# Attention sums of a two-layer graph attention in the next layer's layout: four heads side by side, weight sums repeated over 32 rows

## The chip, the cores and the metric

One Trainium2 chip, one core. The metric is the device time of one execution in microseconds, as the median over runs; lower is better.

## The reference, cut to what matters

Four graphs of 256 nodes go through two graph-attention layers of 8 heads with 32 outputs each, then through a gated residual sum, a layer norm, a router (2 of 16 experts per token) and a mixture of experts with one shared expert.

```python
def gat_layer(x, adj, W, a_self, a_neigh, b):
    feat = jnp.einsum('nf,hfo->hno', x, W)
    e = attn_self[:, :, None] + attn_neigh[:, None, :]
    e = jax.nn.leaky_relu(e, 0.2) + MASK_VAL * (1.0 - adj)[None, :, :]
    alpha = jax.nn.softmax(e, axis=-1)
    out = jnp.einsum('hnm,hmo->hno', alpha, feat) + b[:, None, :]
    return jax.nn.elu(jnp.transpose(out, (1, 0, 2)).reshape(out.shape[1], -1))
...
x = x + jnp.tanh(g_xattn[0]) * gat(gat(ctx, ...), ...)
x = x + jnp.tanh(g_ffn[0]) * moe(_layernorm(x))
```

The softmax's division is made late: the kernel sums weight times feature and weight alone, and divides the one by the other. The elu follows.

## The kernel before, in words

All orders are written out by hand, engine by engine; semaphores join them. A **unit** k is one graph in one layer; `UNITS` lists the four graphs in layer 0 (k = 0 to 3), then the four in layer 1 (k = 4 to 7). The stretch over all units is called the graph stage here. In a unit VectorE makes the terms of 8 heads (`edge(k, h)`, L857, two instructions a head, 128x256 each) out of `ps_edge` into `prob`, a ring of 4 heads. Between two heads `task(k, h)` puts small jobs for the unit before, for the one after, and for the routing of graphs that are done. TensorE has a like order (`task(k, j)`, j counts pairs of heads):

- `edges` (L1198) makes the sums for VectorE's next pair of heads; `rows` (L1165) and `features` (L1174, L1178) belong to units ahead; `spread_t` is L1187.
- `weighted(k, j)` (L1214) sums the terms of two heads. The weights' sum is a 33rd column of `feat`, so a head takes 33 columns of the array; one head stands at column 0 and the other at column 64.
- `turn_pv` (L1225) turns the sums of all heads, after ScalarE (`evict_pv`, L582) has copied them out of `ps_pv`. VectorE's `normalise` takes 16 reciprocals per row (L865) and multiplies (L868); ScalarE's `elu` (L592, L594) and VectorE's `add_elu` (L875) follow. In layer 0 the result is turned again (`turn_z`, L1143 on `att`) and copied out to `h1_t` (`evict_h1`); in layer 1 it is added to `x_res` (L879).

GpSimd multiplies features (L438), takes differences (L423, L461) and later scatters rows (L488) and results (L496). After the graph stage come the routing of the last graphs (`norm_stats`, `hat`, `turn_hat`, `high`, `low`, `route`, `top_two`, `hot`, `ranks`, `positions`), half of the shared expert's steps (`up` L1306, `down` L1316), the table of tiles (`tables`), 31 tiles of routed tokens (L1335, L1346, L1362), the other half of the shared steps, and the collection of results: `bring` (L1063) adds them, `base` (L1029) adds the shared part, and for graph 3 TensorE adds them (L1325).

Of the kernel before, what the change touches and what calls it, by code (L numbers as in the profile page):

```python
# [9 lines left out]
ALU = mybir.AluOpType  # L10
# [3 lines left out]
P = 128  # L14
# [20 lines left out]


def flamingo_block(nc, x, ctx_t, gates, w0, w1, a_self, a_neigh, b0, b1, router_t, router_bias,
# [24 lines left out]
    y_view = [y_tok[Y_SLOTS * P + k * TOKENS:Y_SLOTS * P + (k + 1) * TOKENS, :].rearrange(  # L62
        "(g t p) d -> g p t d", g=B, p=P) for k in range(TOP)]

    with ExitStack() as ctx:
# [6 lines left out]
        def sem(name):  # L72
# [70 lines left out]
        pv_t = sb("pv_t", [P, PAIRS, N])  # L143
        inv_sum = sb("inv_sum", [P, T, HEADS])
# [41 lines left out]


# [13 lines left out]
        y_sb = pv_t  # L201
        y_got = [t[:].rearrange("p a c n -> p (a c n)").rearrange("p (a t d) -> p a t d", a=B, t=T)
                 for t in (prob, mask_t)]
# [6 lines left out]
        ps_mix = ps_nat[:, 0, :]  # L210
        ps_route = ps_feat[:].rearrange("p c f -> p (c f)")
# [13 lines left out]
        down_landed = sem("down_landed")  # L225
# [21 lines left out]
        pv_zeroed, edge_ready, p_done, pv_done = (sem("pv_zeroed"), sem("edge_ready"), sem("p_done"),  # L247
                                                  sem("pv_done"))

        pv_out, pv_turned = [sem(f"pv_out{i}") for i in range(2)], sem("pv_turned")  # L250
        elu_exp = sem("elu_exp")
        z_done, elu_act, elu_sum, z_turned, h1_ready = (sem("z_done"), sem("elu_act"), sem("elu_sum"),
                                                        sem("z_turned"), sem("h1_ready"))
# [20 lines left out]
        y_landed = [[sem(f"y_landed{k}{g}") for g in range(B)] for k in range(TOP)]  # L274
        last_added = sem("last_added")
# [22 lines left out]
        def _(sp):  # L298
# [48 lines left out]
            sp.dma_start(down_w[:, 0:EXPERTS, :], wd).then_inc(down_landed, 16)  # L347
            sp.dma_start(down_w[:, EXPERTS:STEPS, :], sd).then_inc(down_landed, 16)

# [21 lines left out]
            for g in range(B):  # L371
                sp.dma_start(y_got[0][:, g], y_view[0][g]).then_inc(y_landed[0][g], 16)
# [6 lines left out]
        def _(pool):  # L379
# [46 lines left out]
            def scale_features(k):  # L426
# [8 lines left out]
                if k >= 2:  # L435
                    pool.wait_ge(pv_done, PAIRS * (k - 1))
# [3 lines left out]
                                   ).then_inc(feat_ready, 1)  # L440

# [8 lines left out]
            def name_rows(a):  # L450
# [3 lines left out]
                if a == B - 1:  # L454
                    pool.wait_ge(pv_done, PAIRS * NU)
# [51 lines left out]
            for k in range(NU):  # L507
                if graph_after(k - 2, 1) is not None:
                    norm_rstd(graph_after(k - 2, 1))
# [961 lines left out]
```

## Time and profile before

| | us |
|---|---|
| median of 3 runs | 228.59 (228.13 to 230.41) |
| the profiled execution | 228.06 |
| its span | 226.3 |
| graph stage, first to last term of VectorE | 18.46 to 123.53 |
| tiles, from their first turn | 158.35 |
| last instruction of `base` begins | 222.96 |

The span is what the profile covers; 1.76 us of the execution lie around it. In rows of the trace an instruction is given with its line, what it writes and reads, its shape and its time; a PE row's shape begins with the array's rows and columns that it uses.

### The profile page before, as it was taken

What the parts mean: (1) busy time and instruction counts of PE and PEld (TensorE: products, weight loads), DVE (VectorE), ACT (ScalarE), POOL (GpSimd) and SP (SyncE); (2) the same over time, 40 slices, a digit from 0 to 9 for tenths busy, and PEclk for the clock granted to TensorE, in tenths of its full rate; (3) what the DMA queues carried; (4) which work ended last, traced back from release to release, by engine and by line L of the source; (5) the groups of instructions that cost most, each with busy time, mean ns of one, the idle gap of its engine ahead of it and who ended that gap; (6) DMA issues with size and microseconds to landing.
All of it is one profiled execution on the core that took longest, in us unless ns stands there. A gap on an engine that the chain in (4) does not pass through costs nothing.

```text
span 226.3 us, 4159 instructions
## 1 busy us (share of the span) xinstructions
PE 187.1 (83%) x1106; PEld 139.9 (62%) x1106; DVE 167.1 (74%) x506; ACT 116.5 (51%) x313; POOL 109.6 (48%) x140
## 2 busy tenths in 40 slices
PE   0267999899999998698896879288899999999943
PEld 0245555556676666285463679277799999987910
DVE  6946997897979788957997675764677777772455
ACT  2075646958647685564505443000588888885200
POOL 8616771861141847544656235670056666667000
PEclk9999557999999999978558576659999999999995
DMA  3899999999940040880001002225245665642484
GB/s 114 223 242 407 426 424 427 418 433 421 316 138 1 3 139 0 243 311 6 1 23 70 0 3 93 72 93 136 55 133 171 189 184 180 184 136 89 139 295 152
DMA packets 20616, 40.13 MB, mean 177 GB/s; under 512 B 2769, under 2 KB 16658, under 8 KB 18418
## 3 DMA queue, kind: packets, MB, share of 16 engines
q1 hardware_dynamic: 17250, 32.64, 41.5%
q0 software_dynamic: 2256, 6.18, 7.8%
q10 hardware_dynamic: 1088, 1.05, 1.4%
q8 instruction: 10, 0.16, 0.3%
q14 instruction: 12, 0.10, 0.1%
HBM read 15.59 MB, written 24.27 MB: 176 GB/s over the span
## 4 chain that ended last, share of the span: by engine, by line
PE 59%; DVE 19%; ACT 8%; issue 8%; DMA 4%; POOL 0%; DVEq 0%; ACTq 0%; POOLq 0%
PE ps_pv L1214 11%; PE ps_edge L1346 10%; PE ps_pv L1362 6%; DVE prob L857 5%; PE ps_edge L1306 4%; PE ps_edge L1198 4%; PE ps_rows L1165 4%; PE ps_nat L1225 3%; PE ps_pv L1316 3%; PE ps_nat L1143 3%; PE ps_nat L1335 3%; DMA mask_t<-y_tok 3%; PE ps_feat L1178 2%; DVE att L875 2%; PE ps_nat L1187 1%
## 5 line engine op out<-in xcount | busy, mean ns | idle before, releaser
L857 DVE SCALAR_TENSOR_TENSOR prob<-ps_edge,t_nat,mask_t 128x256 f32<-128x256 f32 x128 | 53.7, 474 | 4.1 <-PE ps_edge L1198 1.3
L1214 PE MATMUL ps_pv<-prob,feat 128*33 128x256 f32 x256 | 40.6, 446 | 4.3 <-DVE prob L857 4.2
L496 POOL DMA_INDIRECT y_tok<-pv_t,y_row x31 | 29.7, 959 | 27.6 <-issue 14.6
L461 POOL TENSOR_TENSOR up_lo<-up_raw,up_hi 128x512 fp32r<-128x512 f32 x18 | 23.1, 1296 | 15.1 <-ACT up_hi L619 15.1
L1346 PE MATMUL ps_edge<-up_hi,sel_row 128*128 x124 | 25.9, 301 | 0.8 <-DVE sel_row L1036 0.8
L1214 PEld LDWEIGHTS ps_pv<-prob,feat 128*33 128x33 f32 x256 | 13.8, 123 | 19.1 <-issue 6.6
L1198 PE MATMUL ps_edge<-rows_r,sel_row 128*128 128x256 f32 x64 | 18.0, 374 | 5.5 <-DVE prob L857 5.4
L1198 PEld LDWEIGHTS ps_edge<-rows_r,sel_row 128*128 128x128 f32 x64 | 11.4, 227 | 14.7 <-DVE prob L857 9.0
L1036 DVE TENSOR_TENSOR sel_row<-ps_nat,sel_row 128x256 fp32r<-128x256 f32 x31 | 13.1, 424 | 9.1 <-ACT sel_row L700 9.1
L1346 PEld LDWEIGHTS ps_edge<-up_hi,sel_row 128*128 128x128 f32 x124 | 18.8, 189 | 1.6 <-issue 1.6
L1362 PE MATMUL ps_pv<-down_w,x_less 128*128 x62 | 18.6, 383 | 0.0
L1346 PE MATMUL ps_edge<-up_lo,sel_row 128*128 x62 | 17.4, 280 | 0.0
L423 POOL TENSOR_TENSOR rows_r<-rows_e,rows_h 128x256 fp32r<-128x256 f32 x8 | 5.8, 729 | 23.7 <-ACT rows_h L551 23.7
L582 ACT ACTIVATE pv_t<-ps_pv 128x512 f32<-128x512 f32 x16 | 9.6, 598 | 13.4 <-PE ps_pv L1214 13.4
L718 ACT ACTIVATE pv_t<-ps_pv,mask_t 128x256 f32<-128x256 f32 x31 | 14.7, 474 | 3.3 <-PE ps_pv L1362 0.3
L488 POOL DMA_INDIRECT x_rows<-x_hat,pos x12 | 11.9, 993 | 8.2 <-DVE pos L955 5.4
L1165 PE MATMUL ps_rows<-xc_t,w_rows 65*128 65x256 f32 x16 | 6.9, 578 | 9.8 <-DVE w_rows L812 9.8
L694 ACT ACTIVATE a_all<-ps_edge 128x256 f32<-128x256 f32 x8 | 3.0, 380 | 20.0 <-PE ps_edge L1306 20.0
L700 ACT ACTIVATE sel_row<-ps_nat 128x256 fp32r<-128x256 f32 x31 | 11.6, 378 | 2.5 <-PE ps_nat L1335 2.5
L438 POOL TENSOR_TENSOR feat<-feat_raw,feat 128x512 f32<-128x512 f32 x8 | 8.6, 1073 | 8.5 <-ACT feat_raw L568 8.2
L706 ACT ACTIVATE mask<-ps_edge 128x128 f32<-128x128 f32 x31 | 8.6, 277 | 7.4 <-PE ps_edge L1346 7.4
L1225 PEld LDWEIGHTS ps_nat<-ident,pv_t 128*128 128x128 f32 x64 | 9.0, 172 | 5.3 <-issue 5.3
(186 smaller groups left out, 476.3 us busy)
## 6 DMA issues: line engine op xcount, KB each, us to landing
x_rows<-x_hi SPq DMA_DIRECT2D x16, 1024.0 KB, 22.8
mask_t<-x_rows SPq DMA_DIRECT2D x31, 129.0 KB, 2.1
down_w<-in_wd SPq DMA_DIRECT2D x1, 2048.0 KB, 9.3
up_raw<-in_wu SPq DMA_DIRECT2D x5, 384.0 KB, 6.9
up_raw<-in_wg SPq DMA_DIRECT2D x5, 384.0 KB, 8.0
x_res<-in_x SPq DMA_DIRECT2D x4, 256.0 KB, 3.4
prob<-y_tok SPq DMA_DIRECT2D x4, 256.0 KB, 4.6
mask_t<-y_tok ACTq DMA_DIRECT2D x4, 256.0 KB, 6.8
```

Source lines behind the costliest of these rows:

```text
L461: pool.tensor_tensor(up_lo[:, e], up_raw[:, e % RAW_SLOTS], up_hi[:, e].bitcast(F32), ALU.subtract).then_inc(up_ready, 1)
L488: pool.indirect_dma_start(x_rows[:], bass.IndirectOffsetOnAxis(pos[:, a, k, t:t + 1], 0), rows_of[a][:, k, t, :], None).then_inc(scattered ...
L496: pool.indirect_dma_start(y_tok[:], bass.IndirectOffsetOnAxis(y_row[:, j % R_SLOTS:j % R_SLOTS + 1], 0), y_sb[:, j % Y_SLOTS, :], None).th ...
L718: act.activation(y_sb[:, j % Y_SLOTS], ps_y[j % 2], ACT.Copy, scale=x_in[:, j % X_SLOTS, D + 1:D + 2]).then_inc(y_ready, 1)
L857: last = dve.scalar_tensor_tensor(prob[:, n % 4, c, :], ps_edge[n // 2 % 2][:, h % 2, :], t_nat[:, k % 2, c, 0, h:h + 1], mask_t[:, a, c, ...
L1036: dve.tensor_tensor(xt_lo[:, j % 2], ps_xt[j % 2], xt_hi[:, j % 2].bitcast(F32), ALU.subtract).then_inc(lo_done, 1)
L1165: last = pe.matmul(ps_rows[:, side], w_rows[i][:, c, side, :], src, start=(c == 0), stop=(c == chunks - 1))
L1198: last = pe.matmul(ps_edge[n % 2][:, h % 2, :], sel_row[:, h, :], rows_r[:, k % 2, :], start=True, stop=True)
L1214: last = pe.matmul(ps_pv[at:at + HO, j, :], feat[:, k % 2, c, h, :], prob[:, (HEADS * k + h) % 4, c, :], start=(c == 0), stop=(c == C - 1))
L1225: last = pe.transpose(ps_nat[:, t, j * P:(j + 1) * P], pv_t[:, j, t * P:(t + 1) * P], ident[:])
L1346: last = pe.matmul(to, m[:, j % 2, c, :], w[:, bass.ds(e, 1), :, c * P:(c + 1) * P], start=(i == 0), stop=(i == len(todo) - 1))
L1362: pe.matmul(ps_y[j % 2], ht_r[:, j % 2], down_w[:, bass.ds(e, 1), :], start=True, stop=True).then_inc(y_done, 1)
```

## The change

Four heads stand side by side at columns 0, 32, 64 and 96 (`sums(k, q)`, q counts groups of four). Features' sums and weights' sums become two sets of matmuls; the weights' column is repeated 32 times, so that each weight sum comes out in the same 32 rows as the feature sums that it divides. Nothing is turned: ScalarE copies the feature sums (`evict_sums`), VectorE takes the reciprocal of the whole block of weight sums (`invert`), and GpSimd multiplies the two (`weigh_sums`). For the last unit VectorE does both, in two halves (`normalise_last`). The elu is now max(x, exp(-relu(-x)) - 1) in layer 0, written straight into `h1_t` (`next_layer`), and exp(-relu(-x)) + relu(x) in layer 1, where the two parts are turned and added by TensorE (`turn_elu`) and the -1 stays in `less_gate` as before.

The terms now have 8 places: the second four lie in the half of `down_w` that holds experts 8 to 15, which is loaded only when the last sums are made. The orders of all engines move with this. After the graph stage `norm_stats(2)`, `shared_step(0)`, `positions`, `top_two_in(3)`, `up(1)`, `down(0)` and the scatter of graph 1 change places. Each token's two results lie side by side in `y_tok`, so that one transfer of 512 KB brings a graph's results, and TensorE adds those of graphs 2 and 3.

```diff
+QUAD = 4
+LATE_DOWN = (8, 16)
...
+        terms = [prob[:], down_w[:, LATE_DOWN[0]:LATE_DOWN[1], :].rearrange("p (a c) n -> p a c n", c=C)]
...
+            sp.wait_ge(quad_done, 2 * NU)
+            sp.dma_start(down_w[:, LATE_DOWN[0]:LATE_DOWN[1], :], wd[:, LATE_DOWN[0]:LATE_DOWN[1], :]
+                         ).then_inc(late_down_landed, 16)
...
+            def weigh_sums(k):
+                pool.wait_ge(inv_ready, k + 1)
+                pool.wait_ge(f_sum_out, k + 1)
...
+                pool.tensor_tensor(z[:], f_sum, w_inv, ALU.mult).then_inc(z_done, 1)
...
+            def elu(k, halves=slice(0, 2)):
...
+                act.activation(att[:, halves], z[:, halves], ACT.Relu, scale=-1.0).then_inc(elu_step, 1)
...
+                last = act.activation(att[:, halves], att[:, halves], ACT.Exp, scale=-1.0)
+                if UNITS[k][1] == 1:
+                    last = act.activation(z[:, halves], z[:, halves], ACT.Relu)
...
-            def normalise(k):
-                dve.wait_ge(pv_turned, k + 1)
-                pv = ps_nat[:].rearrange("p t (h o) -> p t h o", h=HEADS)
-                link(dve.reciprocal(inv_sum[:].unsqueeze(3), pv[:, :, :, F_OUT:HO]))
...
+            def invert(k):
+                dve.wait_ge(quad_done, 2 * k + 2)
...
+                dve.reciprocal(w_inv, ps_weight).then_inc(inv_ready, 1)
+            def normalise_last(half):
...
+                link(dve.reciprocal(w_inv[:, half], ps_pv[:, 2 * half + 1]))
+                dve.tensor_tensor(z[:, half], ps_pv[:, 2 * half], w_inv[:, half], ALU.mult).then_inc(z_done, 1)
+            def next_layer(k):
...
+                dve.scalar_tensor_tensor(h1_t[:, a % 2], att[:], -1.0, z[:], ALU.add, ALU.max).then_inc(h1_ready, 1)
...
+            def sums(k, q):
+                pe.wait_ge(p_done, HEADS * k + QUAD * (q + 1))
...
+                for c in range(C):
+                    for h in heads:
+                        at = F_OUT * (h % QUAD)
+                        last = pe.matmul(ps_pv[at:at + F_OUT, to_f, :], feat[:, k % 2, c, h, 0:F_OUT], terms[q][:, h % QUAD, c, :],
+                                         start=(c == 0), stop=(c == C - 1))
+                last.then_inc(sums_done, 1)
...
+                for c in range(C):
+                    for h in heads:
+                        at = F_OUT * (h % QUAD)
+                        last = pe.matmul(ps_pv[at:at + F_OUT, to_w, :],
+                                         feat[:, k % 2, c, h, F_OUT:HO].to_broadcast([P, F_OUT]),
+                                         terms[q][:, h % QUAD, c, :], start=(c == 0), stop=(c == C - 1))
+                last.then_inc(quad_done, 1)
...
+            def turn_elu(k, a):
...
+                        pe.matmul(to, att[:, g, t * P:(t + 1) * P], ident[:], start=True, stop=False)
+                        last = pe.matmul(to, z[:, g, t * P:(t + 1) * P], ident[:], start=False, stop=True)
```

VectorE, unit 3, before: its heads, the next unit's row maxima, and the jobs of unit 2 between heads.

```order
L857 SCALAR_TENSOR_TENSOR prob<-ps_edge0,t_nat,mask_t 128x256 x2
L838 TENSOR_REDUCE row_max<-ps_rows 128x2
L857 SCALAR_TENSOR_TENSOR prob<-ps_edge0,t_nat,mask_t 128x256 x2
L857 SCALAR_TENSOR_TENSOR prob<-ps_edge1,t_nat,mask_t 128x256 x4
L857 SCALAR_TENSOR_TENSOR prob<-ps_edge0,t_nat,mask_t 128x256 x2
L865 RECIPROCAL inv_sum<-ps_nat 128x16
L868 TENSOR_TENSOR z<-ps_nat,inv_sum 128x512
L857 SCALAR_TENSOR_TENSOR prob<-ps_edge0,t_nat,mask_t 128x256 x2
L857 SCALAR_TENSOR_TENSOR prob<-ps_edge1,t_nat,mask_t 128x256 x2
L875 SCALAR_TENSOR_TENSOR att<-att,z 128x512
L844 TENSOR_TENSOR feat<-t_nat 128x16
L857 SCALAR_TENSOR_TENSOR prob<-ps_edge1,t_nat,mask_t 128x256 x2
```

The same after the change (`y_sb` holds `w_inv`; `down_w` is the second four places of terms):

```order
L885 SCALAR_TENSOR_TENSOR prob<-ps_edge0,t_nat,mask_t 128x256 x2
L865 TENSOR_REDUCE row_max<-ps_rows 128x2
L885 SCALAR_TENSOR_TENSOR prob<-ps_edge0,t_nat,mask_t 128x256 x2
L885 SCALAR_TENSOR_TENSOR prob<-ps_edge1,t_nat,mask_t 128x256 x2
L895 RECIPROCAL y_sb<-ps_pv 128x512
L885 SCALAR_TENSOR_TENSOR prob<-ps_edge1,t_nat,mask_t 128x256 x2
L885 SCALAR_TENSOR_TENSOR down_w<-ps_edge0,t_nat,mask_t 128x256 x4
L885 SCALAR_TENSOR_TENSOR down_w<-ps_edge1,t_nat,mask_t 128x256 x2
L911 SCALAR_TENSOR_TENSOR h1_t<-att,z 128x512
L885 SCALAR_TENSOR_TENSOR down_w<-ps_edge1,t_nat,mask_t 128x256 x2
L872 TENSOR_TENSOR feat<-ps_nat,t_nat 128x16
```

The reciprocal has 512 elements a row in place of 16 and stands one head earlier, and the multiplication has left VectorE.

TensorE, unit 4, before:

```order
L1225 MATMUL ps_nat<-ident,pv_t 128x128 x8
L1198 MATMUL ps_edge1<-rows_r,sel_row 128x256 x2
L1214 MATMUL ps_pv<-prob,feat 33x256 x4
L1178 MATMUL ps_feat<-w1_raw,h1_t 128x256 x4
L1187 MATMUL ps_nat<-pick,rows_q 128x24 x2
L1214 MATMUL ps_pv<-prob,feat 33x256 x4
L1198 MATMUL ps_edge0<-rows_r,sel_row 128x256 x2
L1165 MATMUL ps_rows<-h1_t,w1_rows 128x256 x4
L1214 MATMUL ps_pv<-prob,feat 33x256 x4
L1198 MATMUL ps_edge1<-rows_r,sel_row 128x256 x2
L1143 MATMUL ps_nat<-ident,att 128x128 x4
L1198 MATMUL ps_edge0<-rows_r,sel_row 128x256 x2
```

The same after (layer 0 is the unit before, so nothing is turned):

```order
L1236 MATMUL ps_edge0<-rows_r,sel_row 128x256 x2
L1216 MATMUL ps_feat<-w1_raw,h1_t 128x256 x4
L1236 MATMUL ps_edge1<-rows_r,sel_row 128x256 x2
L1254 MATMUL ps_pv<-prob,feat 32x256 x8
L1262 MATMUL ps_pv<-prob,feat 32x256 x8
L1225 MATMUL ps_nat<-pick,rows_q 128x24 x2
L1236 MATMUL ps_edge0<-rows_r,sel_row 128x256 x2
L1203 MATMUL ps_rows<-h1_t,w1_rows 128x256 x4
L1236 MATMUL ps_edge1<-rows_r,sel_row 128x256 x2
L1254 MATMUL ps_pv<-down_w,feat 32x256 x8
L1262 MATMUL ps_pv<-down_w,feat 32x256 x8
```

Both kinds of turn are gone, and the sums come in two blocks of 16 matmuls a unit, the second only behind the unit's last head. In layer 1 eight matmuls of `turn_elu` stand behind the second `edges`.

## Rows read from the trace of the kernel before

**Rows 1.** The span in 40 equal slices (tenths busy, tenths of TensorE's full clock).

```profile
PE   0267999899999998698896879288899999999943
DVE  6946997897979788957997675764677777772455
PEclk9999557999999999978558576659999999999995
```

**Rows 2.** Windows of the eight units (the 4th, the 7th, the 8th) and their sum.

```profile
55.60:65.72 10.12, 10.12 (x70) 6.75 (x69) 9.00 (x22) 6.30 (x17) 2.09 (x3) 1.00 0.90 291
...
91.97:107.49 15.52, 12.40 (x75) 8.30 (x74) 11.58 (x29) 9.22 (x22) 6.94 (x9) 0.83 0.56 194
107.49:123.53 16.04, 12.81 (x63) 7.89 (x59) 14.04 (x46) 6.22 (x12) 9.82 (x12) 0.61 0.09 33
sum 105.07, PE 94.41 PEld 59.96 DVE 89.36 ACT 62.76 POOL 56.12; mean PE 11.80 PEld 7.49 DVE 11.17 ACT 7.85 POOL 7.02
```

**Rows 3.** What VectorE waited for in the graph stage: us in all, times, longest.

```profile
DVE att L875 <- ACT z L594: 4.5, 5, 1.4
DVE x_lo L890 <- ACT x_hi L632: 3.5, 2, 2.4
DVE row_max L838 <- PE ps_rows L1165: 2.0, 3, 0.9
```

**Rows 4.** Timeline of TensorE in units 3 and 4 (start, us, passes merged).

```profile
59.69 1.06 PE L1225 MATMUL ps_nat<-ident,pv_t 128*128 128x128 f32 x8
60.51 0.48 PE L1198 MATMUL ps_edge<-rows_r,sel_row 128*128 128x256 f32 x2
60.92 1.06 PE L1214 MATMUL ps_pv<-prob,feat 128*33 128x256 f32 x8
61.91 1.99 PE L1178 MATMUL ps_feat<-w_raw,h_t 128*128 128x256 f32 x8
63.74 0.52 PE L1187 MATMUL ps_nat<-pick,rows_q 128*128 128x24 f32 x4
...
68.67 0.60 PE L1143 MATMUL ps_nat<-ident,att 128*128 128x128 f32 x4
69.03 0.49 PE L1198 MATMUL ps_edge<-rows_r,sel_row 128*128 128x256 f32 x2
```

**Rows 5.** Groups by line and shape (busy us, mean ns, idle before).

```profile
L438 POOL TENSOR_TENSOR feat<-feat_raw,feat 128x512 f32<-128x512 f32 x8 | 8.6, 1073 | 8.5 <-ACT feat_raw L568 8.2
...
L868 DVE TENSOR_TENSOR z<-ps_nat,inv_sum 128x512 f32<-128x512 f32 x8 | 5.5, 691 | 0.3
...
L865 DVE RECIPROCAL inv_sum<-ps_nat 128x16 f32<-128x16 f32 x8 | 2.0, 255 | 2.7 <-PE ps_nat L1225 2.4
...
L949 DVE TENSOR_TENSOR place<-ps_rows,first_row 128x32 f32<-128x32 f32 x4 | 0.7, 185 | 2.0 <-PE ps_rows L1260 1.4 <-PE ps_rows L1263 0.6
...
L941 DVE RECIPROCAL r_inv<-r_sum 128x2 f32<-128x2 f32 x4 | 0.7, 166 | 0.1
...
L786 DVE TENSOR_SCALAR t_scale<-kind 128x1 f32<-128x1 f32 x1 | 0.1, 134 | 0.0
```

**Rows 6.** Timeline of VectorE, in unit 7 and behind the graph stage.

```profile
117.30 0.69 DVE L868 TENSOR_TENSOR z<-ps_nat,inv_sum 128x512 f32<-128x512 f32 x1
117.90 0.87 DVE L857 SCALAR_TENSOR_TENSOR prob<-ps_edge,t_nat,mask_t 128x256 f32<-128x256 f32 x2
...
131.30 0.75 DVE L879 SCALAR_TENSOR_TENSOR x_res<-att,gate,x_res 128x512 f32<-128x512 f32 x1
...
141.34 0.19 DVE L949 TENSOR_TENSOR place<-ps_rows,first_row 128x32 f32<-128x32 f32 x1 [1.41 <-PE ps_rows L1260]
```

**Rows 7.** Timeline of TensorE at the end.

```profile
219.85 1.13 PE L1325 MATMUL ps_pv<-prob,ident 128*128 128x512 f32 x2 [2.75 <-DMA prob<-y_tok]
221.12 1.70 PE L1325 MATMUL ps_pv<-mask_t,ident 128*128 128x512 f32 x2
```

**Rows 8.** Transfers: KB each, median us to landing.

```profile
down_w<-in_wd SPq DMA_DIRECT2D x1, 2048.0 KB, 9.3
```

More of the change, by code:

```diff
@@ L672, in task @@
                     high(gone)
-                if h == 5 and 0 <= before < NU:
-                    elu(before)
-                if h == 5 and 0 <= after < NU:
+                if after < NU:
                     evict_t(after)
-                if h == 5 and k in MASK_SLOT:
-                    evict_mask(MASK_SLOT[k])
-                if h == 5 and gone is not None:
-                    if after < NU:
-                        high(gone)
-                    copy_hat(gone)
-                if h == 6 and 0 <= after < NU:
+                if gone is not None and after < NU:
+                    high(gone)
@@ L872, in add_elu @@
[L872 to L880 removed]
+                    dve.wait_ge(z_done, k)
@@ L1002, in task @@
                     router_weights()
-                if h == 4 and 0 <= before < NU:
-                    normalise(before)
+                if h == 2 and 0 <= before:
+                    invert(before)
                 if h == (6 if after < NU else 5) and gone is not None:
                     low(gone)
-                if h == 6 and 0 <= before < NU:
-                    add_elu(before)
-                if h == 6 and 0 <= after < NU:
+                if h == 6 and graph_after(before, 0) is not None:
+                    next_layer(before)
+                if h == 7 and after < NU:
                     feature_weights(after)
                 if h == 7 and done is not None:
+                    gated(done)
+                if h == 7 and done is not None and after < NU:
                     norm_stats(done)
@@ L1085, in _ @@
             hot(1)
-            normalise(NU - 1)
+            normalise_last(0)
+            norm_stats(2)
             weigh(1)
-            add_elu(NU - 1)
+            normalise_last(1)
+            positions(1)
+            gated(3)
             norm_stats(3)
             low(2)
-            positions(1)
+            shared_step(0)
             top_two_in(2)
@@ L1277, in task @@
                 gone, routed = graph_after(k - 2, 1), graph_after(k - 3, 1)
[L1278 to L1279 removed]
                 if j == 0 and routed is not None:
                     ranks(routed)
[L1282 to L1284 removed]
+                if j == 0 and after < NU:
                     features(after)
[L1286 to L1288 removed]
+                if j == 1:
+                    if gone is not None:
+                        turn_hat(gone)
+                    sums(k, 0)
+                    if after < NU:
+                        spread_t(after)
+                if j == 2 and graph_after(before, 1) is not None:
+                    turn_elu(before, graph_after(before, 1))
                 if j == 2 and later < NU:
                     rows(later)
+                if j == 2 and k in MASK_SLOT:
+                    turn_mask(MASK_SLOT[k])
                 if j == 2 and gone is not None:
                     route(gone)
[L1293 to L1294 removed]
+                if j == 3:
+                    sums(k, 1)
             def up(s):
```

306 lines of the change are left out of this document (146 added, 160 removed).

## The prediction

> **What bounds the kernel now.** I read the slices first [rows 1]: TensorE is 0.8 to 1.0 busy nearly all through and VectorE is close behind it in the first half. Then I cut the graph stage into its eight units [rows 2]. In unit 3 TensorE is busy for all of its 10.12 us and VectorE for 9.00: TensorE sets the pace, VectorE is 11% away. In unit 7 it is the other way round: VectorE 14.04 of 16.04, TensorE 12.81. Over the stage (105.07 us) TensorE is busy 94.41 and VectorE 89.36, so VectorE has only 15.7 us of idle time. Its largest waits are for ScalarE's elu, 4.5 us, and for the high parts, 3.5 us [rows 3]. This is the point of the case: work taken off TensorE is worth at most the distance to VectorE, and work put on VectorE costs nothing only as long as it fits in 15.7 us.
>
> **TensorE's part in the graph stage.** Removed: `turn_pv`, 59.69 to 60.51 = 0.82 us [rows 4], seven of its eight in the stage, 5.7; `turn_z`, 68.67 to 69.03 = 0.36, four times, 1.4. The sums: a pair of heads is eight passes in 0.99 us (60.92 to 61.91), and a pass over the whole array takes 0.23 (61.91 to 63.74, eight passes) [rows 4]. So eight narrow passes cost what four wide ones do: two heads run at the same time. Four pairs a unit are 3.96. After, a block of four heads has 16 passes for the features and 16 for the weights. If four run at once that is four slots each, 0.87 + 0.87 and some 0.2 of entry and exit, 1.93 a block and 3.9 a unit; with fewer entries, 0.1 less round `edges`, I take a saving of 0.4 a unit, 3.2 in all. Added: `turn_elu`, eight matmuls of two passes over 128 columns, at the 0.10 of a pass in `turn_pv` 1.7 us, three times in the stage, 5.1. TensorE comes to 94.4 - 5.7 - 1.4 - 3.2 + 5.1 = 89.2 us. It gains 5 us, and only units 0 to 4 gain, since in layer 1 `turn_elu` costs more than the turn that goes.
>
> What a row shows of side-by-side work is two heads at 1.75 of one's rate [rows 4]. The Trainium skill, "TensorEngine Tiling (Array Packing)", Tiling Modes, lists 128x32 as four tiles, and "TensorE: Matmul & The Clock Gate", Measured speedup vs the span model, gives 2.38x for three of them. By the list the sum above stands; by the measured efficiency of 0.79 a tile a block costs an estimated 0.4 us more, 6 us over 16 blocks, which VectorE's new work would cover.
>
> **VectorE's part, the term that decides.** `normalise` took 16 reciprocals a row; `invert` takes 512. What does an element cost? The reciprocal of 16 elements takes 255 ns and that of 2 takes 166 [rows 5]: 6.5 ns for each further element. A tensor_tensor on 32 elements from PSUM, with twice the elements, takes only 185, so reading PSUM doesn't explain the 255; and the multiplication that reads the same strided places for 512 elements takes 691, so the stride doesn't either. At 6.5 ns the new one takes 166 + 510 x 6.5 = 3.48 us. Bounds: were the fixed part only the 134 ns of the shortest small instruction, (255 - 134)/16 = 7.6 ns an element, 4.0 us; were it 185, 4.4 ns, 2.4 us; and at the ordinary pace, 0.69 [rows 5]. I take 3.48, since two reciprocals give it and the nearest row of the same size is another operation. The next instruction starts 0.09 before the end of one (117.30 + 0.69 against 117.90) [rows 6], so 3.4 us are added to a unit.
>
> The Trainium skill, "VectorE: DVE Perf Modes", First, the fixed hardware budget, says that the reciprocal runs an iterative divide with a repeat count of 8. Read as eight cycles an element at the page's 0.96 GHz that is an estimated 8.3 ns and 4.4 us, and the forecast would be 7 us later; the rows' 6.5 ns lie under it but on its side.
>
> Per unit VectorE loses the small reciprocal and the multiplication, 0.26 + 0.69 less the overlap, 0.9 us, seven times in the stage, 6.3; in layer 1 the addition of `add_elu`, 0.6, three times, 1.8. `next_layer` costs what that addition did. It gains seven reciprocals, 23.8. Sum: 89.4 - 6.3 - 1.8 + 23.8 = 105.1 us of VectorE work, as long as the whole stage is now. Not all waits vanish: the start of the stage, the high parts for `low`, and handovers stay; half of today's 15.7, 8 us, is my choice (bounds 3 and 15). The stage becomes 113.1 us, **+8.0**. TensorE's 89.2 fit inside, in stretches: it waits for heads 0 to 3 behind the reciprocal, then has a block of sums, `spread_t` and `edges` ready before VectorE needs them two heads later.
>
> **Edits that ride under this.** GpSimd's multiplication takes 1.1 us (the like one over 512 elements is 1.07) [rows 5] and stands ahead of `rows_split`, on which `edges` of the next unit wait; from the reciprocal's end this is 1.1 + 0.7, and TensorE asks for it two or three heads and a block of sums later, some 2.5 us: cover 0.7, and if it is gone the same 0.7 a unit shows. ScalarE does two or three passes of elu in place of two, and has slack (62.8 busy of 105) [rows 2]. Its result is due four heads behind the reciprocal, 3.1 us, and takes 1.1 + 1.3 in layer 0. The late half of `down_w` is 1 MB and, at 9.3 us for 2 MB [rows 8], lands at 136 at the latest; behind it on SyncE's queue stand only tile loads from 155 on. The memset of `ps_pv` lay before the first data.
>
> **Between stage and tiles.** Two half reciprocals, 166 + 254 x 6.5 = 1.8 us each, now stand ahead of graph 3's residual, as does `norm_stats(2)` (1.1); the turns, the eviction and the full-size steps between go. From the last term (123.5) to the residual of graph 3 it is 7.8 us now (131.30) [rows 6]; I count 0.7 gated(2), 2.2 routing of graph 1, 1.8 + 0.4, 1.1, 1.05 weigh, 1.8 + 0.4, 1.2 elu of a half, 0.9 turn, 0.6 handovers, 12.1: +4.3. The new order gives back: `up(1)` (2.6) no longer stands ahead of `route(3)`, and `top_two_in(3)` no longer waits for `positions(2)` at 141.34 [rows 6], 0.7 more. Net **+1.0** (-1 to +3).
>
> **The end.** Today graph 3's second half lands at 221.1 and is added in 1.7 us [rows 7]. After, each graph comes in one transfer with pieces of 4 KB, which nothing in the trace prices; I take a landing 1.8 us earlier, after which both halves are added, 2.0 us in place of 1.7. Two additions leave VectorE. **-1.5** (0 to -3).
>
> **Sum.** 228.06 + 8.0 + 1.0 - 1.5 = 235.6 for the profiled execution; the median lies 0.5 above that, so 236.
>
> **Rivals.**
> - *The reciprocal at ordinary pace (faster).* If 512 reciprocals take 0.69 us, VectorE's stage work is 89.4 - 8.1 + 4.2 = 85.5, TensorE's 89.2 bounds again, with 8 us of waits 97: -8. The two halves behind it take 0.4 each in place of 1.8, so +1.0 becomes -1.8; the end -1.5: 217. For it: every other operation of this trace costs about one ns an element. Against: 255 ns for 16. It decides from about 2.5 us a reciprocal downward, where the 7.5 us of the forecast are spent over eight of them. 0.15.
> - *In between.* 2.4 us each, or nearly all waits absorbed: stage +0.5 to +3, 227 to 230. 0.08.
> - *TensorE's clock.* TensorE now idles behind every reciprocal. In unit 7, where it idles in 3.2 us, the granted clock is 0.61 on average, in unit 3 it is 1.00 [rows 2]. At the lower of its two levels (1.2 GHz) its 9 us of a unit become some 15, above VectorE's 12.5: +2.5 a unit so struck. Three units: 243. 0.12.
> - *Four heads don't run at once, only two* (the change doesn't do what it says). Each block has eight slots more, 1.73 us, 27.7 in all; TensorE 116.9 + 8 = 125: 249. Against: two heads do. 0.05.
> - *The forecast*, 231 to 241: 0.60.
>
> **How the numbers follow.** A measurement of this kernel tells 1% (2.3 us) from nothing. Faster 0.15 is the first rival; same 0.08 is the second; the rest is slower, 0.77. 227 to 247 leaves out the first rival and the fourth, 0.20.
>
> **What would show it.** The 128x512 reciprocal at 3.3 to 3.6 us eight times over (seven whole, two halves); VectorE busy above 0.9 in the units and TensorE below 0.85; the waits of TensorE put down to terms; a block of 16 + 16 passes in 1.8 to 2.0 us; graph 3's residual 12 us behind the last term. A reciprocal near 0.7 us would overturn the forecast's sign; slots of 0.22 us with two starts each would raise it.

## The result, and the profile after

The changed kernel took 253.0 us (median of 4 runs, 248.7 to 256.2) against 229.2 of the kernel before on the same chip: 1.090 times as long, 95% interval 1.076 to 1.103. That is 20 to 24 us more (by the ratio and by the medians), where 7.4 were forecast, and outside the range of 227 to 247. A ratio with an interval is formed from the faster runs of each kernel (those within 1.5% of its fastest), a median from all its runs. The profiled execution was the longest of the four, 256.2 us with a span of 254.5; what of its excess is TensorE's clock is said below.

The graph stage cut into its eight units, changed kernel, with the columns of [rows 2] (length, busy us of TensorE, its weight loads, VectorE, ScalarE, GpSimd, then the granted clock):

```profile
18.58:32.08 13.50, 11.81 (x85) 7.50 (x87) 12.30 (x33) 7.17 (x19) 10.14 (x15) 1.00 1.02 426
32.08:48.48 16.40, 11.39 (x80) 7.07 (x72) 12.28 (x23) 8.02 (x20) 9.47 (x10) 0.68 1.01 426
48.48:66.49 18.01, 15.13 (x104) 9.12 (x100) 11.01 (x20) 7.30 (x19) 5.45 (x6) 0.63 0.90 327
66.49:77.22 10.73, 7.19 (x77) 4.75 (x70) 10.73 (x20) 6.44 (x16) 3.16 (x3) 1.00 0.00 0
...
125.55:140.86 15.31, 8.33 (x78) 4.70 (x70) 14.08 (x41) 6.26 (x12) 5.96 (x7) 0.67 0.01 2
sum 122.28, PE 94.01 PEld 61.62 DVE 96.57 ACT 60.38 POOL 59.87; mean PE 11.75 PEld 7.70 DVE 12.07 ACT 7.55 POOL 7.48
```

The stage is 122.3 us long, 17.2 more than before, where 8.0 were forecast. Unit 3 is the forecast come true: VectorE is busy for all of its 10.73 us and TensorE for 7.19. Unit 2 is not: VectorE has 11.01 us of work, nearly as in unit 3, and the unit takes 18.01, at a granted clock of 0.63. Since VectorE was expected to bound every unit, its idle time is the thing to read. Its waits in the stage (us in all, times, longest), changed kernel:

```profile
DVE prob L885 <- ACT mask_t L647: 9.6, 3, 4.9
DVE feat L872 <- ACT t_nat L599: 4.9, 4, 1.9
DVE x_res L917 <- PE ps_nat L1276: 4.8, 2, 3.6
DVE x_lo L928 <- ACT x_hi L654: 4.1, 2, 3.5
DVE row_max L865 <- PE ps_rows L1203: 2.2, 3, 0.9
```

Together with 0.2 us for the sums VectorE waits 25.7 us: by units, which are length less busy time, 1.2, 4.1, 7.0, 0, 1.6, 5.7, 4.8 and 1.2. Before it was 15.7, the largest single entry 4.5 [rows 3]; 8 were forecast. The reciprocal itself, by line and shape in the whole span (busy us, mean ns, idle before):

```profile
L895 DVE RECIPROCAL y_sb<-ps_pv 128x512 f32<-128x512 f32 x7 | 23.5, 3350 | 0.2 <-PE ps_pv L1262 0.2
L902 DVE RECIPROCAL y_sb<-ps_pv 128x256 f32<-128x256 f32 x2 | 3.5, 1751 | 0.0
L979 DVE RECIPROCAL r_inv<-r_sum 128x2 f32<-128x2 f32 x4 | 0.7, 166 | 0.1
```

From 256 to 512 elements it is 1599 ns more, 6.25 ns an element. That is the forecast's 3.48 us, 4% too long, and not the 255 ns of [rows 5] for 16.

How a wait for the mask comes about is seen in unit 1. First VectorE from the reciprocal on (start, us), then TensorE over the same stretch, changed kernel:

```profile
35.04 3.35 DVE L895 RECIPROCAL y_sb<-ps_pv 128x512 f32<-128x512 f32 x1
38.30 0.78 DVE L885 SCALAR_TENSOR_TENSOR prob<-ps_edge,t_nat,mask_t 128x256 f32<-128x256 f32 x2
...
44.77 0.19 DVE L872 TENSOR_TENSOR feat<-ps_nat,t_nat 128x16 f32<-128x16 f32 x1 [0.56 <-ACT t_nat L599]
48.48 0.88 DVE L885 SCALAR_TENSOR_TENSOR prob<-ps_edge,t_nat,mask_t 128x256 f32<-128x256 f32 x2 [3.53 <-ACT mask_t L647]
```

```profile
39.13 0.80 PE L1236 MATMUL ps_edge<-rows_r,sel_row 128*128 128x256 f32 x2 [3.37 <-DVE prob L885]
39.86 1.94 PE L1254 MATMUL ps_pv<-prob,feat 128*32 128x256 f32 x16
41.57 1.93 PE L1262 MATMUL ps_pv<-prob,feat 128*32 128x256 f32 x16
43.43 1.05 PE L1225 MATMUL ps_nat<-pick,rows_q 128*128 128x24 f32 x4
44.31 0.78 PE L1236 MATMUL ps_edge<-rows_r,sel_row 128*128 128x256 f32 x2
44.88 1.91 PE L1203 MATMUL ps_rows<-xc_t,w_rows 65*128 65x256 f32 x4
46.58 1.06 PE L1181 MATMUL ps_nat<-ident,mask 128*128 128x128 f32 x4
```

TensorE stands still for 3.37 us while VectorE inverts. What it does next it does at the lower of its two levels: 16 narrow passes take 1.94 us here and 1.07 us in unit 3, at granted clocks of 0.68 and 1.00. Its row of work up to the mask's turn ends at 47.6; at the full level the passes of 39.13 to 47.64 would take an estimated 55 to 65% of that (1.07 for 1.94, 0.51 for 0.80). VectorE, out of terms since 45.0, waits 3.53 us for the mask's eviction. So in this unit the reciprocal costs twice: its own length, and a TensorE that comes out of the pause slow.

What the slow TensorE costs is seen best in the changed kernel itself, traced a second time (`after_again`, below). Its stage is 116.3 us long, with the same 96.7 us of VectorE's work. Of the six stretches from one reciprocal to the next four agree to 0.01 us in the two traces. The other two don't, those that begin in units 2 and 5. Here they are (columns as above) in the first trace and then in the second:

```profile
51.71:69.45 17.74, 13.83 (x96) 8.98 (x97) 10.93 (x21) 7.74 (x19) 3.03 (x3) 0.71 0.73 255
93.65:110.82 17.17, 14.77 (x112) 11.19 (x112) 12.24 (x26) 8.33 (x23) 10.63 (x12) 0.80 0.34 106
```

```profile
51.73:66.38 14.65, 10.87 (x96) 7.12 (x97) 10.92 (x20) 7.75 (x19) 3.04 (x3) 0.88 0.87 315
90.57:104.84 14.27, 11.55 (x112) 8.57 (x113) 12.36 (x27) 8.52 (x23) 9.94 (x10) 1.00 0.26 80
```

They differ by 3.1 and 2.9 us, which is the whole difference of the stages, and by the granted clock; VectorE's work is the same to 0.1 us. The clock isn't lowered behind every reciprocal: in the first trace it falls behind five of the seven, in the second behind four; behind that of unit 3 it stays at 1.00 in both, and that of unit 7 finds it low already. The old kernel has such stretches too, without these pauses: 0.68, 0.83, 0.83 and 0.61 in units 0, 1, 6 and 7. In four traces of kernels whose stage is the same or nearly so, VectorE's work is 96.6 or 96.7 us, and the length goes with the granted clock: 122.2 and 122.3 us at 0.80, 119.4 at 0.83, 116.3 at 0.85. With the reciprocals away or on ScalarE (below) it is 93 to 96 us at 0.93 to 0.95, but there VectorE has 18 to 22 us less to do as well.

Behind the stage, distances from the last term of the graph work, us, read from the timelines of the two kernels:

| | before | after |
|---|---|---|
| to graph 3's residual | 7.8 | 16.9 |
| to the first tile's turn | 34.8 | 40.9 |
| first tile's turn to last tile's result | 48.5 | 49.4 |
| last tile's result to the end | 19.4 | 23.3 |

These are one trace each. In `after_again` the residual comes 16.7 us behind the last term, as here, but the first tile's turn 44.1, so that the second row is uncertain by some 3 us.

The last unit on VectorE, changed kernel, timeline:

```profile
142.36 0.75 DVE L917 SCALAR_TENSOR_TENSOR x_res<-ps_nat,gate,x_res 128x512 f32<-128x512 f32 x1 [1.50 <-PE ps_nat L1276]
...
145.70 1.83 DVE L966 TENSOR_TENSOR seen<-seen,both_hot 128x16 fp32r<-128x16 f32 x1
147.45 1.75 DVE L902 RECIPROCAL y_sb<-ps_pv 128x256 f32<-128x256 f32 x1
...
151.72 1.76 DVE L902 RECIPROCAL y_sb<-ps_pv 128x256 f32<-128x256 f32 x1
...
157.72 0.75 DVE L917 SCALAR_TENSOR_TENSOR x_res<-ps_nat,gate,x_res 128x512 f32<-128x512 f32 x1 [2.90 <-PE ps_nat L1276]
```

The two half reciprocals are as forecast. Not forecast: 1.83 us for an addition that takes 0.17 one line earlier, 2.1 us of other work between the two halves, and a turned sum that took TensorE from 154.3 to 157.7, at the lower level (0.63 us for two passes that take 0.39 at 140 us).

### The profile page after: what moved, and what is told of

Same layout as the page of the kernel before. It is cut to its first block, busy times and chain, and to the rows that moved or that the text cites. A ratio compares the mean times of both kernels' runs of the same rounds, so it can differ in the third digit from the quotient of the medians.

```text
span 254.5 us, 4617 instructions
## 1 busy us (share of the span) xinstructions
PE 192.2 (76%) x1350; PEld 144.8 (57%) x1350; DVE 176.9 (70%) x494; ACT 114.8 (45%) x307; POOL 118.6 (47%) x147
## 4 chain that ended last, share of the span: by engine, by line
PE 44%; DVE 24%; issue 15%; DMA 9%; ACT 4%; POOL 3%; DVEq 0%; POOLq 0%; SPq 0%
DVE prob L885 7%; PE ps_edge L1394 7%; PE ps_pv L1262 5%; PE ps_pv L1254 5%; PE ps_pv L1410 4%; PE ps_rows L1203 4%; DMA mask_t<-x_rows 4%; PE ps_edge L1236 3%; PE ps_nat L1225 2%; DMA prob<-y_tok 2%; PE ps_nat L1383 2%; PE ps_nat L1275 2%; PE ps_pv L1374 2%; PE ps_nat L1181 2%; PE ps_nat L1276 2%
## 5 line engine op out<-in xcount | busy, mean ns | idle before, releaser
L515 POOL DMA_INDIRECT y_tok<-y_sb,y_row x31 | 29.7, 958 | 26.8 <-issue 13.6
L1236 PE MATMUL ps_edge<-rows_r,sel_row 128*128 128x256 f32 x64 | 19.2, 391 | 25.9 <-DVE prob L885 25.7
L885 DVE SCALAR_TENSOR_TENSOR prob<-ps_edge,t_nat,mask_t 128x256 f32<-128x256 f32 x64 | 26.5, 466 | 9.6 <-ACT mask_t L647 9.6
L885 DVE SCALAR_TENSOR_TENSOR down_w<-ps_edge,t_nat,mask_t 128x256 f32<-128x256 f32 x64 | 26.3, 474 | 0.0
L459 POOL TENSOR_TENSOR z<-y_sb 128x512 f32<-128x512 f32 x7 | 8.9, 1270 | 37.2 <-DVE y_sb L895 37.2
L895 DVE RECIPROCAL y_sb<-ps_pv 128x512 f32<-128x512 f32 x7 | 23.5, 3350 | 0.2 <-PE ps_pv L1262 0.2
L1410 PE MATMUL ps_pv<-down_w,x_less 128*128 x62 | 18.7, 385 | 0.0
L617 ACT ACTIVATE att<-z 128x512 f32<-128x512 f32 (+1 forms) x9 | 5.2, 583 | 28.2 <-POOL z L459 22.3
L746 ACT ACTIVATE y_sb<-ps_pv,mask_t 128x256 f32<-128x256 f32 x31 | 14.7, 474 | 3.4 <-PE ps_pv L1410 0.5
L1365 PE MATMUL ps_pv<-down_w,a_all 128*128 128x256 f32 x32 | 9.8, 441 | 5.7 <-DVE a_all L1061 5.7
L1262 PE MATMUL ps_pv<-prob,feat 128*32 128x256 f32 x128 | 14.1, 583 | 0.0
L1254 PE MATMUL ps_pv<-prob,feat 128*32 128x256 f32 x128 | 13.0, 543 | 0.0
```

The source lines that it names most:

```text
L515: pool.indirect_dma_start(y_tok[:], bass.IndirectOffsetOnAxis(y_row[:, j % R_SLOTS:j % R_SLOTS + 1], 0), y_sb[:, j % Y_SLOTS, :], None).th ...
L746: act.activation(y_sb[:, j % Y_SLOTS], ps_y[j % 2], ACT.Copy, scale=x_in[:, j % X_SLOTS, D + 1:D + 2]).then_inc(y_ready, 1)
L885: last = dve.scalar_tensor_tensor(terms[h // QUAD][:, h % QUAD, c, :], ps_edge[n // 2 % 2][:, h % 2, :], t_nat[:, k % 2, c, 0, h:h + 1], m ...
L895: dve.reciprocal(w_inv, ps_weight).then_inc(inv_ready, 1)
L1236: last = pe.matmul(ps_edge[n % 2][:, h % 2, :], sel_row[:, h, :], rows_r[:, k % 2, :], start=True, stop=True)
L1254: last = pe.matmul(ps_pv[at:at + F_OUT, to_f, :], feat[:, k % 2, c, h, 0:F_OUT], terms[q][:, h % QUAD, c, :], start=(c == 0), stop=(c == C ...
```

## The experiments

Two theories stood against each other. *Load*: VectorE's reciprocals cost the time, directly or through what they do to TensorE. *Orders*: the new order on ScalarE and behind the stage costs it, and a cheaper inverse would change little. The comparisons were made in four batches on different chips, in which the kernel before had medians of 228.9, 240.4, 241.4 and 240.0 us, so each run is read by its ratio to the kernel before in its own batch, or by stretches of its trace.

**The reciprocals away.**

```diff
-dve.reciprocal(w_inv, ps_weight).then_inc(inv_ready, 1)
+dve.tensor_scalar(w_inv, ps_weight, 0.0, None, ALU.mult).then_inc(inv_ready, 1)
```

(and the same for the two halves)

> The changed kernel with each reciprocal of the weight sums replaced by a multiplication by zero of the same shape (0.7 us for 512 elements), so the division is left out and the attention gives zeros. If the reciprocals' load on VectorE is the cause, 7 x 2.66 + 2 x 1.3 = 21 us go and the kernel comes to 228 to 232. If the new orders cost by themselves (ScalarE's masks behind the elu, the end), most of those 21 us stay and it comes to 238 to 245.

227.0 us, ratio 0.990 (0.985 to 0.995). Some 22 to 26 us are gone, for 21.4 us less of VectorE work (seven times 2.67 and two of 1.33). The windows of the stage in one row each, first this kernel and then, with the altered last unit (below), the same again:

```profile
18.70:115.10 96.40, 80.73 (x734) 55.43 (x734) 78.67 (x207) 59.95 (x142) 60.01 (x63) 0.93 0.57 224
```

```profile
18.60:111.80 93.20, 78.87 (x731) 53.52 (x730) 78.55 (x207) 60.23 (x142) 59.99 (x63) 0.95 0.59 231
```

The stage is 8.7 us shorter than in the kernel before (105.1), though VectorE still waits 17.7 us. So the new layout does gain in the stage. It gives the gain back behind it: 40.1 us from the last term to the first tile's turn, against 34.8.

**The kernel before, with a reciprocal of 512 elements added to each unit** (its result overwritten, so that all results stay).

```diff
+link(dve.reciprocal(z[:], b1_bc[:].unsqueeze(1).to_broadcast([P, T, HF])))
```

> The kernel before with one more reciprocal of 128x512 on VectorE in each of the eight units, from b1_bc into z, ahead of the multiplication that overwrites it; results unchanged. Load theory: 27 us of work on an engine with 15.7 us of idle time in the stage, +12 to +20, 241 to 249. If the reciprocals hide in waits and the orders are the cause, under +6.

252.0 us, ratio 1.106 (1.100 to 1.112). That is the whole loss of the change and a little more, without anything else of it, and 3 us above the upper end of what the load theory had forecast. Its stage, and the row of the added instruction:

```profile
18.70:144.30 125.60, 101.54 (x546) 63.07 (x545) 110.30 (x226) 63.44 (x150) 55.72 (x61) 0.83 0.47 185
```

```profile
L868 DVE RECIPROCAL z<-b_bc 128x512 f32<-128x512 f32 x8 | 26.8, 3353 | 0.3
```

Here VectorE's work grows by 21.0 us and the stage by 20.6: its waits are 15.3 us, where they were 15.7, so the added work filled none of them. The granted clock is 0.83, where the old kernel had 0.85 and, with the new end (below), 0.90. The load theory stands: what decides is the instruction, wherever it is. That it also costs something through TensorE's clock is not seen in this kernel.

**ScalarE's order: the mask's passes ahead of the three passes on z.**

```diff
+if k in MASK_SLOT: mask_exp(MASK_SLOT[k])
 if routed is not None: route_exp(routed)
 ...
 if 0 <= before: elu(before)
-if k in MASK_SLOT: mask_exp(MASK_SLOT[k])
```

> The changed kernel, only ScalarE's order moved: mask_exp stands right behind the row exponentials and ahead of the elu. If the order theory holds, VectorE's 9.6 us of waits for mask_t shrink to under 3 and the time falls by 5 to 10 us, to 243 to 248. If VectorE's load alone is the cause, the waits only move and the time stays within 2 us.

253.2 us, no gain over the changed kernel's 253.0. VectorE's waits for the mask fell from 9.6 to 6.1 us, and the stage to 118.1, at a granted clock of 0.86; at 0.85 the changed kernel itself had 116.3. ScalarE's order alone is not the cause.

**The end.** Two edits: in the changed kernel the first addition of results moved behind the last shared step, and in the kernel before only the new end put in (results of a token side by side, one transfer of 512 KB for a graph, two graphs added on TensorE).

```diff
-bring(0, 0)
 shared_step(SHARED_STEPS - 1)
+bring(0, 0)
 bring(0, 1)
```

```diff
-sp.dma_start(y_got[0][:, g], y_view[0][g]).then_inc(y_landed[0][g], 16)
+sp.dma_start(y_got[g].rearrange("p k f -> p (k f)"), y_view[g]).then_inc(y_landed[g], 16)
 ...
-add_results()
+add_results(2)
+add_results(3)
```

> The changed kernel, only bring(0, 0) moved behind the last shared step on VectorE. If the end is late because the last shared step waits for the first transfer of 512 KB, the 4.0 us wait leaves that step's way and the time falls by 2 to 4 us. If the transfers themselves set the end, it stays within 1 us.

> The kernel before, with only the end of the changed one: the two results of a token side by side in DRAM, one transfer of 512 KB for a graph instead of two of 256 KB, and both results of graphs 2 and 3 added on TensorE. All results as in the kernel before. Transfer theory (the first addition now waits for a transfer twice as long and holds the last shared step behind it, as the changed kernel's trace shows with 4.0 us of wait): the stretch from the last tile's result to the end grows from 19.4 us by 2 to 4 us, and the time comes to 231 to 233 us. Rival (what the changed kernel loses there is due to the lower clock it arrives with): the stretch keeps 18 to 20 us and the time is 227 to 229.5 us.

The first: 250.5 us (244.4 to 255.2), too wide a spread to tell its 2.5 us from nothing; in its trace the stretch at the end is still 23.0 us. The second: ratio 1.003 (0.996 to 1.010), while its trace has 23.0 us there too. Over all traces of this study the new end takes 19.1 to 23.3 us (the changed kernel itself 23.3 and, traced again, 19.6) and the old one 18.7 and 19.4. So one pair of traces can't price it; by the ratio the new end costs at most 1%, and the forecast gain of 1.5 us is not to be seen.

**The inverse on another engine.** ScalarE makes it as exp(-ln w), with both kinds of sums scaled by 2^-40.

```diff
-dve.reciprocal(w_inv, ps_weight).then_inc(inv_ready, 1)
+act.activation(w_inv, ps_weight, ACT.Ln, scale=2.0 ** -40).then_inc(elu_step, 1)
+...
+act.activation(w_inv, w_inv, ACT.Exp, scale=-1.0).then_inc(inv_ready, 1)
```

> The changed kernel, with the seven 512-element reciprocals taken from VectorE: ScalarE makes them, as the exponential of minus the logarithm of the repeated weight sums (the sums scaled by 2^-40 ahead of both). The two 256-element ones behind the last term stay on VectorE. The stage of graph work took 122.3 us with all reciprocals and 96.4 without any. Load theory (VectorE's 3.35 us seven times is what costs): two more passes of 128x512 on ScalarE, some 0.6 to 0.7 us each as its eviction of this size takes, are 9 us of work on an engine that was busy for 60 of the 122 us; the stage comes to 97 to 104 us and the time to 228 to 235 us. Rival (the chain from the sums to the factor of the mask decides, on whichever engine its steps are): ScalarE stands 1.3 us longer ahead of the mask's and t_nat's evictions in each unit, the stage keeps 110 us or more and the time 240 us or more.

257.5 us beside 240.4 of the kernel before, 1.07; the stage 110.2. By these numbers the rival came true (110 us or more, 240 or more): VectorE waits 36.3 us in the stage, at a granted clock of 0.91, most of it for ScalarE. But there was a reason that neither theory had, in ScalarE's groups of that kernel:

```profile
L612 ACT ACT_TABLE_LOAD x7 | 9.0, 1283 | 0.1
L615 ACT ACT_TABLE_LOAD x7 | 9.0, 1283 | 0.1
```

Each unit loads a function table for the logarithm and another for the exponential: 2.57 us ahead of all that ScalarE does in the unit but the eviction of the sums. The Trainium skill, "ScalarE: Activation LUTs", Rules for kernel authors, says that one set holds both functions and needs one load. Loading that set ahead of the stage:

```diff
+act.add_instruction(mybir.InstLoadActFuncSet(..., act_func_set_id=6))
 for k in range(-1, NU):
     slot(k)
```

> ScalarE makes the seven 512-element inverses (exponential of minus the logarithm), as in the run act_invert, whose trace showed two reloads of ScalarE's function table of 1.28 us in each unit, 17.9 us in all, on top of the two passes of 0.6 us. Here one table that holds both functions is loaded once ahead of the graph work, and that of the hyperbolic tangent once behind it. Reload theory: the 2.6 us in each unit stood ahead of the elu's and the mask's passes, act_invert's stage of 110.2 us falls to 98 to 103 us, near the 96.4 us of the kernel without reciprocals, and the time comes 7 to 12 us below that of the changed kernel by more than act_invert's did: some 1.01 to 1.03 times the kernel before. Rival (VectorE's waits on ScalarE's in-order row of passes stay whatever the inverse costs): the stage stays above 106 us and the ratio above 1.05.

240.6 us beside 241.4, from 1.07 to 1.00, a little better than forecast. The stage:

```profile
18.50:112.30 93.80, 77.69 (x727) 53.22 (x727) 74.70 (x200) 67.96 (x156) 59.44 (x63) 0.95 0.59 232
```

VectorE's work is 22 us less than in the changed kernel, TensorE has no pause behind it and works at 0.95, and the stage is as short as with no division at all (96.4 and 93.2). VectorE still waits 19.1 us in it. On the same chip the changed kernel itself:

> The changed kernel itself, so that it and the mended ones are timed on one chip against the kernel before. Ratio 1.08 to 1.10 if the chip makes no difference to it; on a chip whose tile stage is longer for every kernel (59.9 us in place of 49.4 between the first and the last tile, as in the runs of act_invert) 1.07 to 1.09.

263.4 us, 1.09 times the kernel before, with this stage:

```profile
18.60:134.90 116.30, 88.33 (x733) 57.59 (x733) 96.67 (x207) 60.66 (x142) 59.97 (x63) 0.85 0.48 186
```

**Behind the stage.** The order of the last unit altered: graph 2's statistics earlier, both halves divided one behind the other, the turned sum ahead of graph 2's x_hat on TensorE.

```diff
 normalise_last(0)
-norm_stats(2)     # now in unit 7, right behind gated(2)
-weigh(1)
 normalise_last(1)
+weigh(1)
 positions(1)
 ...
 # TensorE
+turn_elu(NU - 1, B - 1)
 turn_hat(2)
-turn_elu(NU - 1, B - 1)
```

> The changed kernel with only the order behind the last term altered: graph 2's row statistics right behind its residual in unit 7, both last normalisations ahead of graph 1's weights and positions, and the last turned sum ahead of graph 2's x_hat on TensorE. Order theory: the second half is divided 2 us earlier (it stood behind 0.7 and 1.2 us of other work) and the turned sum no longer stands behind x_hat's turn, so that graph 3's residual comes 13 to 14 us behind the last term instead of 16.9, and the time falls by 2 to 4 us, to 249 to 251. Rival (the chain of reciprocal, multiply, three passes on ScalarE and the turned sum, with TensorE at its lower clock, sets it): 16 to 17 us as before and 252 to 254 us.

> The kernel without reciprocals (a multiplication by zero in their place, so the division is left out) and with the order behind the last term altered. Without reciprocals graph 3's residual came 16.1 us behind the last term and the first tile's turn 40.1 us behind it, against 7.8 and 34.8 of the kernel before; with the reciprocals and the altered order 15.0 and 39.8. If the loss behind the stage is the order's, both fall: 12 to 13.5 us to the residual and 36.5 to 38 to the turn. If it is the layout's (two blocks of sums, two halves of z, three passes on ScalarE for each half, a turned sum of 16 passes, one behind the other), it stays at 14 us or more and 39 or more.

With the reciprocals: 259.6 us beside 240.4, 1.08 against the changed kernel's 1.09, which is within the spread; the residual of graph 3 came 15.0 us behind the last term (16.9), the first tile's turn 39.7 (40.9). Without them: 235.7 us beside 241.4, 0.98; 13.4 and 39.1 (16.1 and 40.1). The residual comes as the order theory asks, the turn as the layout theory does: the order is worth some 2.5 us at the residual. The 1 us at the first tile is less than two traces of one kernel differ by (40.9 and 44.1).

All mendings in one, first with the two table loads a unit and then with one table:

> The three mendings in one: the reciprocals on ScalarE, the order behind the last term altered, the mask's passes ahead of the three passes on z in ScalarE's order, and the first addition of results behind the last shared step. If the losses are separate, the time is that of the kernel with ScalarE's reciprocals (228 to 235 expected) less 2 to 4 for the order and 1 to 3 for the end, 223 to 231 us, and may be below the kernel before at 229. If they cover each other, it is within 1 us of the former kernel's.

> The run act_one_table with the order behind the last term altered, the mask's passes first and the first addition of results behind the last shared step. The candidate for a kernel ahead of both: the stage is forecast at 97 to 102 us and the stretch from the last term to the first tile's turn at 38 to 40 us, against 105.1 and 34.8 of the kernel before, so 3 to 5 us are gained in the one and 3 to 5 lost in the other: a ratio of 0.98 to 1.01. If the stretch behind the stage keeps 41 us and the end its 4, 1.01 to 1.03.

Ratios 1.070 (1.060 to 1.080) and, by medians, 236.2 to 241.4, 0.98. That was a miss for the first, which was to reach the kernel before; the table loads were not known when it was written. The second was run again beside a further order of the last unit. That one leaves the mask's passes where the changed kernel has them, and besides the cut below puts the turned sum ahead of graph 1's ranks on TensorE and `norm_rstd(3)` ahead of graph 1's scatter on GpSimd:

```diff
 # unit 7, last head
+invert_half(0)
 gated(done)
 norm_stats(done)
 # behind it
+multiply_half(0)
 top_two_in(1)
 top_two(1)
+invert_half(1)
+multiply_half(1)
 hot(1)
 weigh(1)
-positions(1)
 gated(3)
 norm_stats(3)
+positions(1)
```

> ScalarE's inverse with one table, the first addition of results behind the last shared step, and a new order in the last unit: VectorE inverts the first half of the weights while it waits for graph 2's turned sum (2.7 us of wait in one_table_mended), multiplies it right behind graph 2's statistics, inverts and multiplies the second half ahead of graph 1's one-hot work, and the turned sum stands ahead of graph 1's ranks on TensorE. Order theory: graph 3's residual comes 11 to 12.5 us behind the last term (15.4 in one_table_mended, 17.0 in act_one_table, 7.8 in the kernel before), the first tile's turn 38 to 40 us behind it (43.7, 41.6 and 34.8), and the ratio to the kernel before falls to 0.95 to 0.98. Layout theory: the residual comes earlier, but the ranks and the table behind it don't, the turn stays at 41 us or more and the ratio at 0.98 to 1.0.

> The run one_table_mended again, on one chip with last_unit_split and in more rounds, since its 236.2 us stood against 241.4 us of the kernel before with 234.7 to 243.1 us among that one's runs. If the cheap inverse makes the changed layout the faster one: 0.97 to 0.99 with the interval below 1. If the earlier median was chance: 0.99 to 1.01.

Ratios 0.981 (0.974 to 0.987) and 0.979 (0.971 to 0.986). The medians over all runs differ less, 237.2 and 239.2 beside 240.0, which is 1.1% and 0.3%. So both are as fast as the kernel before or up to 2% faster, and not distinguishable from each other. Against the changed kernel the gain is 10% (236.2 beside 263.4 us in the batch that had both). In last_unit_split graph 3's residual comes 11.8 us behind the last term, as the order theory had it; the first tile's turn comes 41.5 behind it, as the layout theory had it. So the 5 to 6 us between the last term and the tiles don't hang on when that residual is there. No order tried brought them below 39, against 34.5 and 34.8 in two traces of the old layout (38.2 in the one with added reciprocals). What holds them was not settled.

## Why the prediction was wrong

**Right: the direction and the main mechanism.** VectorE's reciprocals decide. Their price was forecast at 3.48 us from two reciprocals of 2 and 16 elements and measured at 3.35 (the two rows, 166 and 255 ns, give 6.4 ns an element and not the 6.5 of the prediction, and so 3.41 us); the lower bounds of 2.4 and 0.69 and the two rivals built on them fell with it. The Trainium skill, "VectorE: DVE Perf Modes", First, the fixed hardware budget, gives its iterative divide a repeat count of 8. That points the right way, but read as eight cycles an element it makes the estimate of 4.4 us, a third too much. The trace decides; its 6.25 ns would be six cycles at the page's 0.96 GHz.

**Right: TensorE's block of four heads.** 16 + 16 passes start 0.89 us apart at the full level (143.49 and 144.38) and end in 1.94 us, forecast 1.93. Four heads do run at once: 16 narrow passes in 0.89 us are four times 0.22, and a pass over the whole array takes 0.23. The list of four tiles in the Trainium skill, "TensorEngine Tiling (Array Packing)", Tiling Modes, holds here. The loss of an estimated 0.4 us a block, which the prediction had worked out from the 2.38x for three tiles in the Trainium skill, "TensorE: Matmul & The Clock Gate", Measured speedup vs the span model, does not show.

**Wrong, the step that failed: "Not all waits vanish ... half of today's 15.7, 8 us, is my choice" in VectorE's part.** The waits were 25.7 us (19.6 in the second trace, at the higher clock). Two things are in that miss of 17.7.

First, new work on VectorE filled no waits. The kernel before with added reciprocals shows it: 21.0 us more work, and 15.3 us of waits in place of 15.7. The halving had no row behind it. Nor are the new orders free of waits of their own: with no reciprocals at all VectorE waited 17.7 us at a granted clock of 0.93, for masks, t_nat, the turned sums and the high parts.

Second, TensorE's clock, 6.0 us between two traces of the same kernel. The step took TensorE's 89.2 us to "fit inside, in stretches", a sum at an unchanged clock. But the 3.4 us in which VectorE gives no terms are a pause for TensorE, and behind four or five of the seven it works at the lower level, so that masks, t_nat and the turned sums come late in the very units that the reciprocal had already lengthened. That was written down as a rival, "TensorE's clock", with a chance of 0.12. Its time of 243 is already the forecast's 236 with 2.5 us for each of three units on top; what was wrong is to treat it as an alternative. In both traces of the changed kernel the forecast's mechanism brought it along, and it belonged in the sum. Even 243 is 3 us under the lower end of the changed kernel's ratio (1.076, 247 us), since it too halves the old waits.

How much of the 25.7 is the clock's beyond those 6.0 us, and how much the orders', is open: no run held the clock up with the reciprocals in place.

**Wrong in size, and hiding a part of it: VectorE's work.** Forecast 105.1 us in the stage, measured 96.6. The addition of layer 0 became cheaper too (0.89 to 0.68 us, four times), the three of layer 1 cost 0.89 and not 0.6 each, and some small instructions, which took 0.53 us on average in the old kernel (its weights of the features), took 0.18 where one of their two operands is now read from PSUM. These are 4 us of the 8.5; the rest is small differences, not followed up. So the forecast of the stage, 113.1, was too low by 9.2 out of two errors, -8.5 in the work and +17.7 in the waits.

**"Between stage and tiles", +1.0: measured +6.1.** The list up to graph 3's residual (12.1) missed 4.8 us. VectorE waited 1.5 us for graph 2's turned sum and 0.5 for graph 1's routing sums, one small addition took 1.83 in place of 0.17, and the turned sum, at the lower level and behind x_hat's turn, ended 2.5 us behind the last pass of elu (155.1 to 157.7) in place of 0.9; against that stand the 0.6 that were put in for handovers. The 3.3 us that the new order was to give back behind the residual came as 3.0 in this trace. The order explains at most about 1 us at the first tile, which is within what two traces of one kernel differ by; the rest is the layout's or open.

**"The end", -1.5:** nothing, within 1%. The larger transfers land 6.2 to 8.4 us behind their issue, where those of 256 KB took 4.6 to 6.8.

**The edits that ride under this** did ride: GpSimd's multiplication took 1.27 us (1.1 forecast) and ScalarE had slack. What their section left out is that ScalarE works in order, and that its passes on z, now behind the reciprocal and GpSimd, stand ahead of the mask's. It was worth 3.5 us of waits and no time in the experiment.

## What to carry to other kernels

When an operation is repeated over a broadcast to save a turn, price it by the element on the engine that gets it: here 16 divisions a row became 512, at 6.25 ns each, and the layout that gained 9 to 12 us in the stage without its divisions lost 20 in all with them. The same layout with the division on ScalarE is level with the old kernel or up to 2% faster, once its two functions share a table. Don't let new work fill an engine's waits in a sum before a row shows that those waits would go: 21 us put on VectorE made the old kernel's stage 20.6 longer. And a long instruction that stops the supply of TensorE can cost its length and then TensorE's lower clock on the work behind, here 3 us a time where it struck: add the two, don't weigh them against each other.

## What the runs showed of the hardware that was not expected

- TensorE's granted clock made the same stretch of the same kernel 3 us longer in one trace than in another, twice in a stage; the four other stretches between reciprocals agreed to 0.01 us.
- The reciprocal on VectorE: 166 ns for 2 elements, 1751 for 256, 3350 for 512, the same in SBUF (3353) and from PSUM.
- A table load on ScalarE is 1283 ns each time. Two of them stood in each unit of act_invert, and none in the units of act_one_table, where the one set was loaded by hand.
- Small instructions of VectorE take 0.17 us or, now and then, ten times that: 1.83 us for `seen` at 145.70, and 0.98 for a cast of 16 elements in one_table_mended. Both end 0.05 us behind the end of a GpSimd pass over 512 elements (`up_lo`, 146.21 to 147.48, and 120.46 to 121.73). That GpSimd's pass is the cause was not tested.
- The tile stage, which no edit touched, took 48.5 to 50.4 us in the first traces and 58 to 61 on the chips of the three later batches, for every kernel. Its cause was not looked for.
